# DLRM tower on one Trainium2 core: pairwise products in units of 64 samples instead of 32

## The chip, the cores and the metric

One core of one Trainium2 chip. The time is the device time of one execution in microseconds; the median over several runs counts, and less is better.

## The reference

2048 samples, each with 128 dense features and 26 ids into 26 tables of rows of 128 numbers. All in fp32. Per sample, the 26 looked-up rows and the dense row are multiplied with one another, and the products go through three layers:

```python
e = jnp.stack([tbl_0[ids[:, 0]], ..., tbl_25[ids[:, 25]]], axis=1)     # (2048, 26, 128)
sd = jnp.einsum('bfd,bd->bf', e, dense)                                # 26 products with the dense row
ss = jnp.einsum('bfd,bgd->bfg', e, e)
pairs = ss[:, iu, ju]                                                  # 325 pairs above the diagonal
z = jnp.concatenate([dense, sd, pairs], axis=1)
h = jnp.concatenate([z, dense], axis=1)                                # 607 columns
h = jnp.maximum(h @ W_top1 + b_top1, 0.0)                              # 512
h = jnp.maximum(h @ W_top2 + b_top2, 0.0)                              # 256
y = h @ W_top3                                                         # 1
```

## The kernel before

The 2048 samples are 16 tiles of 128, in four chunks of four tiles (`CHUNKS`). The last chunk (`LAST`) has an order of its own, written out by hand, in which its two halves (`EARLY`, `FINAL`) go through the layers one after the other.

Rows reach the core in two ways. Seventeen tables are **gathered**: POOL (GpSimd) issues one indirect DMA for each tile and table (L552), 16 x 17 = 272 in all, into the ring `rows` of 44 rows of 128 x 128. A tile takes 18 of them: the dense row, which SP loads, and 17 gathered ones. Before a gather overwrites a ring row, POOL waits until PE has turned it (`rows_turned`). The nine tables of 1000 rows are **looked up** by matmul: DVE makes one-hot columns from the ids (`one_hots`, L1113 in the first chunk, L1115 after it), into four slots, and PE multiplies them with a high and a low part of the table (`look_up`, L576 and L577), 72 blocks of two matmuls for each chunk, one chunk ahead.

PE turns a tile's rows by transposing them, four at a time, into two PSUM banks (`turn_rows`, L597), one tile ahead of the products. DVE or ACT copies them into `turned` (`copy_rows`, L403) and places the looked-up rows there too (`place_found`, L417). Then PE makes the products: for each group of four samples, four matmuls of 27 x 26 (`products`, L616), which write four strips of one PSUM bank. A **unit** is eight groups, 32 samples, 32 matmuls, 8 x 26 = 208 columns of the 512 of a bank; in the profile its matmuls have two records each. A tile has four units, which alternate between the banks `gram_bank0` and `gram_bank1`. `copy_products` (L374) brings a unit into `gram`: DVE from the one bank, ACT from the other. PE waits for that copy before it writes the bank again (`gram_copied`), and the copy waits for the unit (`gram_done`).

The order of the first three chunks is that of the loops `work_off`, one on each engine. On PE each of the 4 x 4 steps (tile `t`, step `u`) is: turn a share of the next tile's rows, make unit `u`, look up three or four blocks for the following chunk. `first_products` makes the very first unit of a chunk ahead of this loop. After the 16 steps PE turns the products by feature (`turn_products`, L644), which waits for all copies of `gram`, then turns the pairs by sample (`turn_pairs`, L657) and runs layers 1 and 2 (L664, L710), with further lookups and the first turns of the following chunk in between. Each engine works strictly in its written order. The waits count events from the start of the program, so `UNITS` (four units to a tile) stands in every one of those counts.

Of the kernel before, what the change touches and what calls it, by code (L numbers as in the profile page):

```python
# [65 lines left out]
UNIT = 8  # L66
UNITS = GROUPS // UNIT
COLS_TURNS = -(-LATER // TURN)
# [63 lines left out]
def turns_before(u):  # L132

    return range(-(-u * TURNS // UNITS), min(-(-(u + 1) * TURNS // UNITS), TURNS))

# [23 lines left out]
def dlrm_tower(nc, dense, ids, ids_t, tables, w1, b1, w2, b2, w3, out):  # L159
# [11 lines left out]
    with ExitStack() as ctx:  # L171
# [189 lines left out]
        def copy_products(engine, chunk, n):  # L361


            mine = int(engine is nc.scalar)
            copy = nc.scalar.copy if mine else nc.vector.tensor_copy
            if chunk.n == 0 and n < 2:

                engine.wait_ge(w2_lo_made, 1)
                engine.wait_ge(w1_lo_made, K1)

            engine.wait_ge(gram_done, chunk.first * UNITS + n + 1)
            of = gram_bank[mine][0:ACROSS, 0:UNIT * LATER].rearrange("p (k f) -> p k f", k=UNIT)
            room = n % (HALF * UNITS) if chunk is LAST else n
            copy(gram[0:ACROSS, room * UNIT:(room + 1) * UNIT, :], of).then_inc(gram_copied[mine], 1)  # L374
# [30 lines left out]
        def place_found(engine, chunk, t):  # L405
# [6 lines left out]
            if t >= 2:  # L412

                engine.wait_ge(gram_done, (chunk.first + t - 1) * UNITS)
# [143 lines left out]
        def _(pe):  # L558
# [41 lines left out]
            def products(chunk, t, u):  # L600
# [9 lines left out]
                n = t * UNITS + u  # L610

                pe.wait_ge(gram_copied[n % 2], UNITS + (chunk.first * UNITS + n) // 2)
                for k in range(UNIT):
                    for q in range(GROUP):
                        sample = turned[:, t % 2, u * UNIT + k, q * FEATURES:(q + 1) * FEATURES]
                        last = pe.matmul(gram_bank[n % 2][q * QUAD:q * QUAD + FEATURES, k * LATER:(k + 1) * LATER],  # L616
                                         sample, sample[:, 0:LATER], start=True, stop=True)
                last.then_inc(gram_done, 1)

            def turn_products(part, g):  # L620

                if g == 0:

                    for i in range(2):
                        pe.wait_ge(gram_copied[i], UNITS + (part.first + part.tiles) * UNITS // 2)
# [127 lines left out]
            def work_off(chunk, following):  # L753
# [3 lines left out]
                for t in range(TILES):  # L757
                    for u in range(int(t == 0), UNITS):
                        if t + 1 < TILES:
                            turn_rows(chunk, t + 1, turns_before(u))  # L760
                        products(chunk, t, u)
# [139 lines left out]
        def _(act):  # L901
# [50 lines left out]
            def work_off(chunk, following):  # L952
                for t in range(TILES):
                    for u in range(UNITS):
# [6 lines left out]
                        if u % 2:  # L961
                            copy_products(act, chunk, t * UNITS + u)
# [133 lines left out]
        def _(dve):  # L1096
# [52 lines left out]
            def work_off(chunk, following):  # L1149
                for t in range(TILES):  # L1150
                    for u in range(UNITS):
                        if u % 2 == 0:
                            copy_products(dve, chunk, t * UNITS + u)
# [159 lines left out]
```

## Time and profile before

| | |
|---|---|
| runs (three) | 378.31 us median, 378.0 to 378.87 |
| span of the profiled execution, first to last instruction | 376.5 us |
| median of the runs beside that span | 1.8 us more |
| PE matmul busy | 347.3 us, 92% |
| PE weight loads (beside the matmuls) | 273.7 us, 73% |
| DVE busy | 252.4 us, 67% |
| ACT busy | 187.5 us, 50% |
| POOL busy | 267.1 us, 71% |
| mean granted TensorE clock | 0.982 of 2.4 GHz |

The record lists no time of its own for the profiled execution beside its span. Busy time leaves out the issue of instructions and waiting. A row of the timeline gives start, duration, engine, line, operation, tiles and shapes; the bracket behind it is the engine's idle time just before, and what ended it. Where several instructions of one kind follow one another, they are one row with their count.

### The profile page before, as it was taken

To read this page: it belongs to the slowest core of one execution; us is meant where nothing else is said; L and a number is where in the kernel's file an instruction comes from. 1 tells how busy PE (TensorE), PEld (TensorE's weight loads), DVE (VectorE), ACT (ScalarE), POOL (GpSimd) and SP (SyncE) were. 2 spreads that over 40 slices of the span, in tenths; PEclk is the share of its full clock that TensorE was granted. 3 is DMA by queue.
4 is the path that set the end of the run, shared out by engine and by line. 5 is a ranking of instruction groups with operands and counts; after the bars stand their busy time and mean duration, and the time that the engine had idled before them with its cause. 6 is when DMAs were issued, how large, how long until landed. Compare 5 with 4: busy or idle time off the path is not lost.

```text
span 376.5 us, 12740 instructions
## 1 busy us (share of the span) xinstructions
PE 347.3 (92%) x5585; PEld 273.7 (73%) x5585; DVE 252.4 (67%) x501; ACT 187.5 (50%) x320; POOL 267.1 (71%) x279
## 2 busy tenths in 40 slices
PE   2899988999799999998999999986899999989987
PEld 0566666876578888876788888864678778779876
DVE  0799899886589735787788646884588672545241
ACT  3356777677113426767323347574214345524443
POOL 6777778777777777777777777777777777877200
PEclk9999999999899999999999999999899999969999
DMA  7998114333242332333432331342243221122100
GB/s 191 256 256 201 51 49 106 94 85 112 67 111 77 85 84 57 86 88 97 111 81 84 78 91 51 87 119 71 75 104 91 51 62 51 52 51 52 31 4 1
DMA packets 20111, 33.43 MB, mean 89 GB/s; under 512 B 7917, under 2 KB 10491, under 8 KB 20057
## 3 DMA queue, kind: packets, MB, share of 16 engines
q0 software_dynamic: 8704, 17.84, 18.4%
q1 hardware_dynamic: 11353, 14.78, 15.0%
q8 instruction: 44, 0.72, 0.8%
q14 instruction: 10, 0.08, 0.1%
HBM read 32.60 MB, written 0.01 MB: 87 GB/s over the span
## 4 chain that ended last, share of the span: by engine, by line
PE 70%; POOL 13%; issue 7%; DMA 5%; DVE 4%; ACT 1%; SPq 0%; DVEq 0%; ACTq 0%; POOLq 0%
POOL rows L552 13%; PE late_bank L576 10%; PE late_bank L664 10%; PE gram_bank L616 8%; PE late_bank L577 8%; PE turn_bank L597 6%; DMA rows<-in_tbl_dram,index 4%; PE gram_bank L576 3%; PE spare_bank L710 3%; PE gram_bank L577 3%; PE spare_bank L576 2%; PE spare_bank L880 2%; PE spare_bank L577 2%; PE turn_bank L577 1%; PE turn_bank L576 1%
## 5 line engine op out<-in xcount | busy, mean ns | idle before, releaser
L552 POOL DMA_INDIRECT rows<-in_tbl_dram,index x272 | 266.3, 979 | 83.9 <-issue 80.5
L1115 DVE TENSOR_TENSOR one_hot<-table_ids,row_number 125x512 fp32r<-125x512 int32 x216 | 134.8, 682 | 30.8 <-PE gram_bank L577 13.1
L403 ACT COPY turned<-turn_bank 128x512 f32<-128x512 f32 (+1 forms) x69 | 68.3, 1033 | 49.0 <-PE turn_bank L597 49.0
L576 PE MATMUL late_bank<-one_hot,table_hi 125*128 125x512 f32 x168 | 72.1, 429 | 1.9 <-DVE one_hot L1113 1.0
L577 PE MATMUL late_bank<-one_hot,table_lo 125*128 125x512 f32 x168 | 67.6, 403 | 0.0
L616 PEld LDWEIGHTS gram_bank<-turned 128*27 128x27 f32 x4096 | 45.3, 106 | 18.7 <-issue 14.1
L616 PE MATMUL gram_bank<-turned 128*27 128x26 f32 x4096 | 55.0, 193 | 2.3 <-DVE turned L417 1.4
L597 PE MATMUL turn_bank<-ident,rows 128*128 128x128 f32 x288 | 44.1, 277 | 12.5 <-DMA rows<-in_tbl_dram,index 11.5
L597 PEld LDWEIGHTS turn_bank<-ident,rows 128*128 128x128 f32 x288 | 35.1, 143 | 23.0 <-DMA rows<-in_tbl_dram,index 14.2
L576 PEld LDWEIGHTS late_bank<-one_hot,table_hi 125*128 125x128 f32 x168 | 32.5, 194 | 16.5 <-issue 5.3
L1113 DVE TENSOR_SCALAR one_hot<-looked_up,row_number_sb 125x512 fp32r<-125x512 f32 x72 | 32.8, 496 | 11.5 <-issue 6.3
L577 PEld LDWEIGHTS late_bank<-one_hot,table_lo 125*128 125x128 f32 x168 | 32.6, 194 | 6.1
L929 ACT ACTIVATE h_hi<-late_bank,b_sb 128x512 fp32r<-128x512 f32 (+1 forms) x18 | 11.1, 617 | 36.7 <-PE late_bank L664 29.9
L374 DVE COPY gram<-gram_bank 124x208 f32<-124x208 f32 x32 | 12.0, 374 | 25.6 <-PE gram_bank L616 25.4
L1146 DVE TENSOR_TENSOR h_lo<-late_bank,h_hi 128x512 fp32r<-128x512 f32 (+1 forms) x18 | 10.8, 599 | 25.2 <-ACT late_bank L929 25.2
L374 ACT COPY gram<-gram_bank 124x208 f32<-124x208 f32 x32 | 11.3, 354 | 32.4 <-PE gram_bank L616 32.1
L664 PE MATMUL late_bank<-input_hi,w_hi 117*128 117x512 f32 (+3 forms) x72 | 27.2, 378 | 0.1
L664 PE MATMUL late_bank<-input_hi,w_lo 117*128 117x512 f32 (+3 forms) x72 | 25.8, 359 | 0.0
L664 PE MATMUL late_bank<-input_lo,w_hi 117*128 117x512 f32 (+3 forms) x72 | 25.8, 358 | 0.0
L417 ACT COPY turned<-looked_up 128x1152 f32<-128x1152 f32 x10 | 23.9, 2394 | 0.0
L576 PE MATMUL spare_bank<-one_hot,table_hi 125*128 125x512 f32 x48 | 21.4, 445 | 0.3 <-DVE one_hot L1115 0.2
L576 PE MATMUL gram_bank<-one_hot,table_hi 125*128 125x512 f32 x48 | 19.5, 407 | 0.2 <-DVE one_hot L1115 0.2
(138 smaller groups left out, 460.5 us busy)
## 6 DMA issues: line engine op xcount, KB each, us to landing
table_ids<-in_ids_by_table_dram SPq DMA_DIRECT2D x27, 256.0 KB, 3.3
rows<-in_tbl_dram,index POOLq DMA_INDIRECT x272
turned<-in_tbl_dram SPq DMA_DIRECT2D x6, 448.0 KB, 12.1
looked_up<-in_tbl_dram SPq DMA_DIRECT2D x3, 448.0 KB, 5.6
rows<-in_r_dense_features_dram SPq DMA_DIRECT2D x16, 64.0 KB, 3.2
gram<-in_W_top_dram SPq DMA_DIRECT2D x1, 702.0 KB
gram<-in_W_top_dram SPq DMA_DIRECT2D x1, 512.0 KB
turned<-in_tbl_dram SPq DMA_DIRECT2D x6, 52.0 KB
```

The costliest lines, as they stand in the source:

```text
L374: copy(gram[0:ACROSS, room * UNIT:(room + 1) * UNIT, :], of).then_inc(gram_copied[mine], 1)
L403: copy(to[:, f0:f1], of).then_inc(rows_copied[n % 2], 1)
L417: copy(to, of).then_inc(placed, 1)
L552: pool.indirect_dma_start(out=rows[:, row % RING_ROWS, :], out_offset=None, in_=tables[f], in_offset=bass.IndirectOffsetOnAxis(ap=index[:, ...
L576: pe.matmul(bank, table_hi[:, s, k, :], hot, start=k == 0, stop=False)
L577: pe.matmul(bank, table_lo[:, s, k, :], hot, start=False, stop=k == K_ROWS - 1).then_inc(one_hot_used, 1)
L597: last = pe.transpose(turn_bank[n % 2][:, f - f0, :], rows[:, (tile * ROWS + f) % RING_ROWS, :], ident[:])
L616: last = pe.matmul(gram_bank[n % 2][q * QUAD:q * QUAD + FEATURES, k * LATER:(k + 1) * LATER], sample, sample[:, 0:LATER], start=True, stop ...
L664: last = pe.matmul(h1_bank(part, n), w[0:p, k, cols], x[0:p, k, samples_of(part)], start=k == 0 and x is input_hi and w is w1_hi, stop=k = ...
L710: last = pe.matmul(h2_bank(part, n), w[:, k, n * P:(n + 1) * P], h1_slot(x, part, k), start=k == 0 and x is h1_hi and w is w2_hi, stop=k = ...
L1113: last = nc.vector.tensor_scalar(hot, id_slot(s), row_number_sb[:, k:k + 1], None, ALU.is_equal)
L1115: last = nc.vector.tensor_tensor(hot, table_ids[0:RK, (chunk.n * LOOKUPS + s) % ID_SLOTS, 0:wide], row_number[0:RK, k:k + 1].broadcast_to( ...
```

## The change

In the first three chunks a unit becomes 16 groups: 64 samples, 64 matmuls, 416 columns of a bank. A tile has two units. The first goes to `gram_bank0` and is copied by DVE, the second to `gram_bank1` and is copied by ACT. PE makes the first in step `u` = 0 and the second in step `u` = 2; the steps 1 and 3 keep their turns and lookups. `LAST` keeps units of 32 samples. `products_before(tile)` counts the units up to a tile, for the waits.

```diff
+WIDE = 2
...
+def wide(chunk):
+
+    return 1 if chunk is LAST else WIDE
+
+
+def products_before(tile):
+
+    return min(tile, LAST.first) * UNITS // WIDE + max(tile - LAST.first, 0) * UNITS
...
-            engine.wait_ge(gram_done, chunk.first * UNITS + n + 1)
-            of = gram_bank[mine][0:ACROSS, 0:UNIT * LATER].rearrange("p (k f) -> p k f", k=UNIT)
+            engine.wait_ge(gram_done, products_before(chunk.first) + n + 1)
+            unit = UNIT * wide(chunk)
+            of = gram_bank[mine][0:ACROSS, 0:unit * LATER].rearrange("p (k f) -> p k f", k=unit)
             room = n % (HALF * UNITS) if chunk is LAST else n
-            copy(gram[0:ACROSS, room * UNIT:(room + 1) * UNIT, :], of).then_inc(gram_copied[mine], 1)
+            copy(gram[0:ACROSS, room * unit:(room + 1) * unit, :], of).then_inc(gram_copied[mine], 1)
...
-                n = t * UNITS + u
-
-                pe.wait_ge(gram_copied[n % 2], UNITS + (chunk.first * UNITS + n) // 2)
-                for k in range(UNIT):
+                unit = UNIT * wide(chunk)
+                n = t * (GROUPS // unit) + u
+
+                pe.wait_ge(gram_copied[n % 2], UNITS + (products_before(chunk.first) + n) // 2)
+                for k in range(unit):
                     for q in range(GROUP):
-                        sample = turned[:, t % 2, u * UNIT + k, q * FEATURES:(q + 1) * FEATURES]
+                        sample = turned[:, t % 2, u * unit + k, q * FEATURES:(q + 1) * FEATURES]
...
                         if t + 1 < TILES:
                             turn_rows(chunk, t + 1, turns_before(u))
-                        products(chunk, t, u)
+                        if u % WIDE == 0:
+                            products(chunk, t, u // WIDE)
                         look_up(following, blocks_after("unit", t, u))
...
-                        if u % 2:
-                            copy_products(act, chunk, t * UNITS + u)
+                        if u == WIDE:
+                            copy_products(act, chunk, t * UNITS // WIDE + 1)
...
-                        if u % 2 == 0:
-                            copy_products(dve, chunk, t * UNITS + u)
+                        if u == 0:
+                            copy_products(dve, chunk, t * UNITS // WIDE)
```

The first piece moved stands on PE, in the third chunk, from the last turn ahead of its fourth tile. `turn_bank` takes turned rows, `gram_bank` products, `late_bank` a lookup's sum; the brackets name semaphores waited for. Before:

```order
L597 MATMUL turn_bank1<-ident,rows 128x128 [waits rows_copied1,gathered2_4]
L597 MATMUL turn_bank1<-ident,rows 128x128
L616 MATMUL gram_bank1<-turned 27x26 [waits gram_copied1]
L616 MATMUL gram_bank1<-turned 27x26 x31
L576 MATMUL late_bank0<-one_hot,table_hi 128x512 [waits one_hot_made]
L577 MATMUL late_bank0<-one_hot,table_lo 128x512
L576 MATMUL late_bank0<-one_hot,table_hi 128x512 [waits one_hot_made]
L577 MATMUL late_bank0<-one_hot,table_lo 128x512
L576 MATMUL late_bank0<-one_hot,table_hi 128x512 [waits one_hot_made]
L577 MATMUL late_bank0<-one_hot,table_lo 128x512
L616 MATMUL gram_bank0<-turned 27x26 [waits found_placed,gram_copied0,rows_copied1,rows_copied0]
L616 MATMUL gram_bank0<-turned 27x26 x31
```

Changed (the lines of the file have moved by 12 to 14):

```order
L609 MATMUL turn_bank1<-ident,rows 128x128 [waits rows_copied1,gathered2_4]
L609 MATMUL turn_bank1<-ident,rows 128x128
L588 MATMUL late_bank0<-one_hot,table_hi 128x512 [waits one_hot_made]
L589 MATMUL late_bank0<-one_hot,table_lo 128x512
L588 MATMUL late_bank0<-one_hot,table_hi 128x512 [waits one_hot_made]
L589 MATMUL late_bank0<-one_hot,table_lo 128x512
L588 MATMUL late_bank0<-one_hot,table_hi 128x512 [waits one_hot_made]
L589 MATMUL late_bank0<-one_hot,table_lo 128x512
L629 MATMUL gram_bank0<-turned 27x26 [waits found_placed,gram_copied0,rows_copied1,rows_copied0]
L629 MATMUL gram_bank0<-turned 27x26 x63
```

The unit between the turn and the lookups is gone, its 32 matmuls now stand in the unit before, and the next tile's first unit has 64.

The second piece is ACT in the third chunk's first tile: copies of turned rows (L403, then L415), of products (L374, then L386), and the placing of looked-up rows (L417, then L429). Before:

```order
L403 COPY turned<-turn_bank1 128x4x4x32 [waits rows_turned,dense_split]
L374 COPY gram<-gram_bank1 124x208 [waits gram_done]
L417 COPY turned<-looked_up 128x9x4x32 [waits found_copied]
L403 COPY turned<-turn_bank0 128x4x4x32 [waits rows_turned,dense_split]
L403 COPY turned<-turn_bank1 128x2x4x32 [waits rows_turned,dense_split]
L374 COPY gram<-gram_bank1 124x208 [waits gram_done]
```

Changed:

```order
L415 COPY turned<-turn_bank1 128x4x4x32 [waits rows_turned,dense_split]
L429 COPY turned<-looked_up 128x9x4x32 [waits found_copied]
L415 COPY turned<-turn_bank0 128x4x4x32 [waits rows_turned,dense_split]
L386 COPY gram<-gram_bank1 124x416 [waits gram_done]
L415 COPY turned<-turn_bank1 128x2x4x32 [waits rows_turned,dense_split]
```

The two copies of products are one, behind the placing and one copy of rows.

The third piece is DVE in the third chunk's second tile, copies of products among one-hots. Before:

```order
L374 COPY gram<-gram_bank0 124x208 [waits gram_done]
L1115 TENSOR_TENSOR one_hot<-table_ids,row_number 125x512 [waits one_hot_used] x4
L1115 TENSOR_TENSOR one_hot<-table_ids,row_number 125x512 [waits one_hot_used,ids_loaded2]
L1115 TENSOR_TENSOR one_hot<-table_ids,row_number 125x512 [waits one_hot_used] x3
L374 COPY gram<-gram_bank0 124x208 [waits gram_done]
L1115 TENSOR_TENSOR one_hot<-table_ids,row_number 125x512 [waits one_hot_used] x4
```

Changed:

```order
L386 COPY gram<-gram_bank0 124x416 [waits gram_done]
L1129 TENSOR_TENSOR one_hot<-table_ids,row_number 125x512 [waits one_hot_used] x4
L1129 TENSOR_TENSOR one_hot<-table_ids,row_number 125x512 [waits one_hot_used,ids_loaded2]
L1129 TENSOR_TENSOR one_hot<-table_ids,row_number 125x512 [waits one_hot_used] x7
```

The second copy is gone, and twelve one-hots follow the first without a copy between them.

## Rows read from the trace of the kernel before

**Rows 1.** The page: busy shares, and the chain that ended last, by engine.

```profile
PE 347.3 (92%) x5585; PEld 273.7 (73%) x5585; DVE 252.4 (67%) x501; ACT 187.5 (50%) x320; POOL 267.1 (71%) x279
...
PE 70%; POOL 13%; issue 7%; DMA 5%; DVE 4%; ACT 1%; SPq 0%; DVEq 0%; ACTq 0%; POOLq 0%
```

**Rows 2.** Waits of POOL's gathers: us in total, times, longest.

```profile
POOL rows L552 <- issue: 80.5, 264, 0.3
POOL rows L552 <- PE turn_bank L597: 2.1, 7, 0.3
```

**Rows 3.** POOL in order of time: the first and last of 272 gathers.

```profile
2.68 1.10 POOL L552 DMA_INDIRECT rows<-in_tbl_dram,index  x1 [1.28 <-DMA index<-in_ids_dram]
...
350.65 0.95 POOL L552 DMA_INDIRECT rows<-in_tbl_dram,index  x1 [0.30 <-issue]
```

**Rows 4.** PE in order of time: turns that waited for gathers, and the last turn.

```profile
178.26 0.66 PE L597 MATMUL turn_bank<-ident,rows 128*128 128x128 f32 x4 [0.80 <-DMA rows<-in_tbl_dram,index]
...
265.07 1.09 PE L597 MATMUL turn_bank<-ident,rows 128*128 128x128 f32 x4 [3.57 <-DMA rows<-in_tbl_dram,index]
...
328.69 0.66 PE L597 MATMUL turn_bank<-ident,rows 128*128 128x128 f32 x4 [0.91 <-DMA rows<-in_tbl_dram,index]
...
331.23 0.69 PE L597 MATMUL turn_bank<-ident,rows 128*128 128x128 f32 x2 [1.21 <-DMA rows<-in_tbl_dram,index]
...
353.35 0.38 PE L597 MATMUL turn_bank<-ident,rows 128*128 128x128 f32 x2
```

**Rows 5.** The chain that ended last: its last piece that is not PE's, before 331.

```profile
328.65 2.53 DMA rows<-in_tbl_dram,index
```

**Rows 6.** Busy time by stretch (us; busy of each engine; PEclk; DMA share; GB/s).

```profile
331.30:353.40 22.10, 22.09 (x450) 20.12 (x451) 9.47 (x29) 9.57 (x30) 15.72 (x16) 0.87 0.21 54
353.40:376.50 23.10, 18.87 (x377) 16.16 (x375) 6.24 (x24) 9.32 (x32) 0.00 (x0) 1.00 0.01 3
```

**Rows 7.** PE in order of time, first chunk's fourth tile: lookup, unit, next unit.

```profile
105.98 0.39 PE L576 MATMUL late_bank<-one_hot,table_hi 125*128 125x512 f32 x1
106.21 0.40 PE L577 MATMUL late_bank<-one_hot,table_lo 125*128 125x512 f32 x1
106.54 0.98 PE L616 MATMUL gram_bank<-turned 128*27 128x26 f32 x64
...
109.04 0.98 PE L616 MATMUL gram_bank<-turned 128*27 128x26 f32 x64
```

**Rows 8.** PE in order of time: the last two units of the program.

```profile
357.23 0.40 PE L616 MATMUL gram_bank<-turned 128*27 128x26 f32 x26
357.79 1.02 PE L616 MATMUL gram_bank<-turned 128*27 128x26 f32 x96 [0.15 <-issue]
```

**Rows 9.** The page's costliest groups: one-hots and copies (busy us, mean ns | idle before).

```profile
L1115 DVE TENSOR_TENSOR one_hot<-table_ids,row_number 125x512 fp32r<-125x512 int32 x216 | 134.8, 682 | 30.8 <-PE gram_bank L577 13.1
...
L374 DVE COPY gram<-gram_bank 124x208 f32<-124x208 f32 x32 | 12.0, 374 | 25.6 <-PE gram_bank L616 25.4
...
L374 ACT COPY gram<-gram_bank 124x208 f32<-124x208 f32 x32 | 11.3, 354 | 32.4 <-PE gram_bank L616 32.1
```

**Rows 10.** DVE's copies of looked-up rows and the gathers under them; the four gathers' sum.

```profile
145.15 1.53 DVE L417 COPY turned<-looked_up 128x1152 f32<-128x1152 f32 x1 [1.04 <-ACT looked_up L914]
...
145.82 1.35 POOL L552 DMA_INDIRECT rows<-in_tbl_dram,index  x1 [0.30 <-issue]
...
323.96 1.89 POOL L552 DMA_INDIRECT rows<-in_tbl_dram,index  x1 [0.30 <-issue]
...
324.59 1.37 DVE L417 COPY turned<-looked_up 128x1152 f32<-128x1152 f32 x1
...
sum 6.80, POOL 6.21; mean POOL 1.55
```

**Rows 11.** Busy time by stretch, columns as in rows 6.

```profile
330.00:333.40 3.40, 2.19 (x70) 1.70 (x70) 1.61 (x4) 0.85 (x3) 2.75 (x3) 0.50 0.27 63
178.30:184.00 5.70, 5.70 (x179) 4.41 (x180) 4.07 (x9) 2.69 (x4) 4.17 (x6) 1.00 0.38 105
```

More of the change, by code:

```diff
@@ L412, in place_found @@
             if t >= 2:
-                engine.wait_ge(gram_done, (chunk.first + t - 1) * UNITS)
+                engine.wait_ge(gram_done, products_before(chunk.first + t - 1))
             to = turned[:, t % 2].rearrange("p i (q f) -> p f q i", q=GROUP)[:, ROWS:FEATURES]
@@ L624, in turn_products @@
                     for i in range(2):
-                        pe.wait_ge(gram_copied[i], UNITS + (part.first + part.tiles) * UNITS // 2)
+                        pe.wait_ge(gram_copied[i], UNITS + products_before(part.first + part.tiles) // 2)
                 if part.tiles == TILES:
```

## The prediction

> **What bounds the kernel now.** I read the share of busy time first, then what POOL (GpSimd) waits for, then POOL in order of time, and last the chain that ended last. The shares seem to name TensorE (PE): busy 92% of the span, and 70% of the chain [rows 1]. That is misleading. POOL issues 272 indirect gathers, one table row per sample each, and its waits say that 80.5 us of its idle time, 264 times at most 0.3 us, is "issue", the gap ahead of nearly every gather; only seven gaps, no longer than the others, are put down to PE [rows 2]. So a gather takes 0.95 us and 0.30 us of gap, and nothing holds POOL up from the first gather at 2.68 to the last at 350.65 us [rows 3]. 271 times 1.25 is 339 us; the other 9 us are longer gathers, spoken of below.
>
> PE runs after the gathers. It waits for rows at 178.26 us (second chunk) and at 265.07 us (third), and in the last chunk at 328.69 (0.91 us) and 331.23 us (1.21 us) [rows 4]. The chain says the same near its end: it comes down POOL's gathers to the one issued at 328.65 us, whose landing takes 2.53 us [rows 5], and from there it is PE. From 331.3 us on PE is busy 22.09 of 22.10 us until it turns the last gathered rows at 353.35 us, and the last 23.1 us hold nothing of the first three chunks [rows 4, 6].
>
> So the end is set by two things: **when the gather of 328.65 us is issued**, and the 45.3 us (331.23 to 376.5) of the last chunk's work behind its landing. The change edits neither.
>
> **The change, part by part.**
>
> *Fewer switches on PE.* In 12 tiles, four units of 32 products become two of 64: 24 fewer. In a tile without turns one unit starts at 106.54 and the next at 109.04 us: 2.50 us for a unit and six lookup matmuls [rows 7]. Before the unit, lookup matmuls follow one another at 0.23 us (six of them 1.40), so a unit costs 1.10 us; the gap ahead of it is 0.10 of that, 0.33 us after the last lookup instead of 0.23. Joining two units saves at least that gap, 0.10 us: the products themselves stay. The other end is from the place where two units already stand nearly side by side: 26 and 96 records in 1.58 us [rows 8], which is 1.66 us for the 128 of a pair, against 2 x 1.10 = 2.20: 0.54 us. I take 0.4, nearer to that row, because it is the same instruction in the same order. 24 times 0.4 is **9.6 us of PE** (2.4 to 13.0). All of it lies ahead of a wait for gathers. Three joined pairs stand behind the wait at 265.07 us; they save 1.2 us (0.3 to 1.6) and bring PE that much earlier to the rows of 328.69 and 331.23 us, so the two waits grow from 2.12 to about 3.3 us. On the time: 0.
>
> *Fewer, wider copies.* 24 copies of 208 columns by VectorE (DVE) at 0.374 us and 24 by ScalarE (ACT) at 0.354 become 12 and 12 of 416 columns [rows 9]. Their cost is not shown: no less than the old one, no more than twice it (0.75 and 0.71 us). I take the middle, 0.56 and 0.53: DVE and ACT save about 2 us each in three chunks, off the path. What waits for a copy: the next unit into the same bank, now a tile later, and the turn of the products behind the last tile, whose second unit is now made one step earlier. On DVE the copy stands ahead of the one-hots. Where eight lookups now follow one unit, PE wants the eighth one-hot behind seven lookups (seven times 0.47) and a turn of rows (0.66, as at 178.26 us [rows 4]): 3.9 us after the unit. Four one-hots are ready by then; the copy and four more take at most 0.75 + 4 x 0.68 = 3.5 us [rows 9]. So no new wait follows, and a small one would be paid from the 3.3 us above.
>
> *Order on ACT.* The copy of the second unit goes behind the placing of looked-up rows and two copies of turned rows. The placing needs looked-up rows and the tile before; nothing waits that did not. SP and POOL keep their order.
>
> **The sum.** The profiled execution has a span of 376.5 us; 0 from PE and 0 from the copies leave 376.5. The median of the runs, 378.31, is 1.8 us above that span; I carry this over: **378.3 us**. The three runs spread over 0.87 us, so 0.2% (0.76 us) is about what can be told from no change.
>
> **What can still move the end: the gathers' own pace.** Behind 62 us nearly all long gathers lie under DVE's copy of looked-up rows into `turned`. Four of these copies come ahead of 328.65 us; the gathers under them took 6.21 us together, 2.41 above four times 0.95 [rows 10]. The gather of 145.82 us began 0.67 us into the copy and took 1.35 (0.40 over); that of 323.96 had run for 0.63 us when the copy began and took 1.89 (0.94 over). The change leaves these copies alone, but PE reaches each about a microsecond earlier, which shifts them against POOL's period of 1.25 us. If all four came out like the cheap one: 1.60, the end 0.8 us earlier; all like the dear one: 3.76, the end 1.35 us later. They average 0.60 now, close to the middle (0.67), so I put the shift at 0.
>
> By the Trainium skill (SBUF — State Buffer, "Who interferes with whom") a DVE copy in a two-port mode blocks GpSimd for the whole instruction; at 1.37 us of copy for each of the four that would be up to 5.48 - 2.41 = 3.1 us later. No gather here lost more than 0.94, so the rows decide.
>
> **The rivals.**
>
> 1. *The gathers fall under DVE's copies* (slower). Place: the four copies above, one at the start of each of the last three chunks and one in the last chunk's middle. Price: up to +1.35 us, **379.7 us**. It decides once the four cost 3.17 us together (0.79 each). For it: one of the four is at the dear end, and all four move. Against: they would have to move the same way. 0.12. The same mechanism at its cheap end gives **377.5 us**: 0.06.
>
> 2. *PE really is the bound* (faster). Then the whole 9.6 us would show: **368.7 us**. For it: 92% busy, 70% of the chain. Against: POOL without a break, and PE waiting for rows in every chunk. 0.06.
>
> 3. *The longer waits cost TensorE its clock* (slower). During the waits of the last chunk the granted clock fell to 0.50, the 1.2 GHz level [rows 11], and behind 331.3 us it still averaged 0.87 over 22.1 us [rows 6], which is 5.7 us at the low level, 2.9 us of PE's work lost; it rose while PE was turning products without a gap. After the shorter wait at 178.26 us it stayed at 1.00 [rows 11]. If the low stretch began at 331.23 itself and not at 330.0, 1.2 us more would lie there: +0.6. If a like stretch came once more behind the last gather: +2.9. **379 to 381 us**. Against: what lies before 331.23 us is paid by waiting, and the work that resumes there is unchanged. Nothing is to be had the other way: the last gather, issued at 350.65 and landing 2.53 us later like the other, is there at 353.18, and PE at 353.35, so a clock that never fell would gain 0.17 us. 0.06.
>
> A rule of the Trainium skill speaks against the change here: by TensorE: Matmul & The Clock Gate, "HAM oscillation — how this bites in real kernels", bursts of matmuls parted by waits for DMA each run at the low clock. Were that so at every wait for gathers, rival 3 would be the likeliest; the full clock after 178.26 us speaks against it.
>
> **How the numbers follow.** No difference that can be told 0.70, gathers dearer 0.12, cheaper 0.06, PE the bound 0.06, clock 0.06. Faster by over 0.2%: 0.06 + 0.06 = 0.12. Slower: 0.12 + 0.06 = 0.18. The forecast's own band is 378.3 within 0.75. The range, 377.4 to 379.3, adds the cheap end of the gathers and most of the dear one; it leaves out rival 2 and the far ends of 1 and 3, together some 0.15.
>
> **What the new profile would show.** POOL unbroken, its idle time still "issue", its last gather within 1.3 us of 350.65. Units of 128 matmul records in 12 tiles, and a pair 0.1 to 0.5 us shorter than two units were. PE's waits for gathers longer by some 8 us in all, the two of the last chunk about 3.3 us together. The chain still on POOL's gathers ahead of 331 us. The prediction is wrong if POOL's stream ends over a microsecond earlier, if PE no longer waits near 331 us, or if the last 45 us have grown.

## The result, and the profile after

The changed kernel takes **380.43 us** (median of 22 runs), the kernel before on the same chip 378.32: ratio 1.0046, interval [1.0027, 1.0064]. The median is 2.1 us higher and the ratio says 0.46% slower, where no difference was forecast; the time is outside the range. Medians here and below are of all runs, while ratios leave out runs over 1.5% above the fastest of the same kernel (here 1719.87, 384.95 and 382.73 us). Without that of 1719.87 us, whose cause is not known, the runs spread from 377.0 to 385.0 us, where before had 377.2 to 379.3. The profiled execution has a span of 378.0 us, 1.5 more than before.

The page, with the shares, the chain and the groups that answer to [rows 1, 9]:

```profile
PE 345.5 (91%) x5585; PEld 274.9 (73%) x5585; DVE 249.5 (66%) x489; ACT 185.7 (49%) x308; POOL 266.8 (71%) x279
...
PE 87%; issue 6%; DVE 4%; ACT 1%; DMA 0%; SPq 0%; DVEq 0%; ACTq 0%
...
L629 PE MATMUL gram_bank<-turned 128*27 128x26 f32 x4096 | 55.0, 193 | 13.0 <-issue 8.7
...
L386 DVE COPY gram<-gram_bank 124x416 f32<-124x416 f32 (+1 forms) x20 | 10.1, 503 | 24.0 <-PE gram_bank L629 24.0
...
L609 PE MATMUL turn_bank<-ident,rows 128*128 128x128 f32 x288 | 44.3, 279 | 0.4 <-ACT turned L415 0.4
```

The same groups of TensorE before, from the list by line:

```profile
L616 PE MATMUL gram_bank<-turned 128*27 128x26 f32 x4096 | 55.0, 193 | 2.3 <-DVE turned L417 1.4
...
L597 PE MATMUL turn_bank<-ident,rows 128*128 128x128 f32 x288 | 44.1, 277 | 12.5 <-DMA rows<-in_tbl_dram,index 11.5
```

Three things are to be read here. PE is busy 1.8 us less, as it should be, but idle 3.3 us more (32.5 us in place of 29.2): that is the 1.5 us. The idle time ahead of the turns, 12.5 us and nearly all of it waits for gathers, is gone (0.4 us are left); in its place 13.0 us stand ahead of the products, where 2.3 were, and 8.7 of them are "issue", time in which PE waited for nothing that the profile shows. And POOL, 13% of the chain before, is no longer on it, although it works as before: its waits (L564 is the gather) and its last gather, which answer to [rows 2, 3], are

```profile
POOL rows L564 <- issue: 82.0, 269, 0.3
```

```profile
350.53 0.95 POOL L564 DMA_INDIRECT rows<-in_tbl_dram,index  x1 [0.30 <-issue]
```

So PE has become the bound. Where its new gaps lie, the order of time on PE shows. A unit of 64 samples has 128 records of L629; four of the 24 are broken:

```profile
74.31 1.39 PE L629 MATMUL gram_bank<-turned 128*27 128x26 f32 x112
...
77.97 0.31 PE L629 MATMUL gram_bank<-turned 128*27 128x26 f32 x16 [2.27 <-issue]
...
167.31 1.37 PE L629 MATMUL gram_bank<-turned 128*27 128x26 f32 x108
...
170.66 0.35 PE L629 MATMUL gram_bank<-turned 128*27 128x26 f32 x20 [1.98 <-issue]
...
180.00 0.61 PE L629 MATMUL gram_bank<-turned 128*27 128x26 f32 x49 [1.63 <-issue]
...
265.16 0.40 PE L629 MATMUL gram_bank<-turned 128*27 128x26 f32 x27 [2.01 <-issue]
...
359.59 1.02 PE L629 MATMUL gram_bank<-turned 128*27 128x26 f32 x96 [0.78 <-issue]
```

The fifth gap is in the last two units of the program, which the change leaves alone; it is the 0.15 us of [rows 8], grown to 0.78.

What happened in the first gap is told by the transfers of that moment. The page lists a queue of its own for "instruction": 44 transfers, 0.72 MB, so 16 KB each. TensorE's stream has 5585 matmul and 5585 weight-load records and some 180 waits; that is 258 of them to a transfer, so about 256 instructions to a **piece** of the program. The DMA view of 71.9 to 75.5 us has no packet of this queue, that of 75.5 to 78.0 us has one:

```profile
q8 instruction: 1, 0.02, 2.3%
```

In the records behind this row the transfer starts at 75.56 us; PE goes on at 77.97, 2.41 us later. Counted from the program's start in instructions, all five gaps stand at place 192 or 193 of 256, where a new piece begins. For each of these pieces the time from the start of its transfer to its first product is 2.25 to 2.51 us. **Theory A** is therefore: a product takes four instructions (two records, two weight loads), a joined unit 256 of them in 1.6 us at the pace of the first row above (1.7 to 2.1 us as units come, the broken ones apart); that is a whole piece in less time than the next one needs to arrive. Before, 128 instructions were followed by lookups, a matmul each 0.23 us [rows 7], and pieces arrived under them. Of 33 transfers between 60 and 310 us, 23 started behind the start of a lookup matmul before and 4 behind that of a product; now 16 of 32 start behind that of a product. **Rival B** is that the copies do it (a bank that is released late, VectorE or ScalarE in another order).

### The profile page after: what moved, and what is told of

Same layout as the page of the kernel before. It is cut to its first block, busy times and chain, and to the rows that moved or that the text cites. A ratio compares the mean times of both kernels' runs of the same rounds, so it can differ in the third digit from the quotient of the medians.

```text
span 378.0 us, 12716 instructions
## 1 busy us (share of the span) xinstructions
PE 345.5 (91%) x5585; PEld 274.9 (73%) x5585; DVE 249.5 (66%) x489; ACT 185.7 (49%) x308; POOL 266.8 (71%) x279
## 4 chain that ended last, share of the span: by engine, by line
PE 87%; issue 6%; DVE 4%; ACT 1%; DMA 0%; SPq 0%; DVEq 0%; ACTq 0%
PE gram_bank L629 14%; PE late_bank L677 11%; PE late_bank L588 11%; PE late_bank L589 10%; PE turn_bank L609 8%; PE spare_bank L588 4%; PE spare_bank L723 3%; PE spare_bank L589 3%; PE gram_bank L588 3%; PE gram_bank L589 3%; PE spare_bank L894 2%; DVE one_hot L1129 2%; PE row_number L723 2%; PE late_bank L735 1%; PE turn_bank L588 1%
## 5 line engine op out<-in xcount | busy, mean ns | idle before, releaser
L564 POOL DMA_INDIRECT rows<-in_tbl_dram,index x272 | 266.0, 978 | 84.1 <-issue 82.0
L415 ACT COPY turned<-turn_bank 128x512 f32<-128x512 f32 (+1 forms) x69 | 68.7, 1037 | 49.3 <-PE turn_bank L609 48.4
L589 PE MATMUL late_bank<-one_hot,table_lo 125*128 125x512 f32 x168 | 69.1, 412 | 1.1 <-issue 1.1
L629 PE MATMUL gram_bank<-turned 128*27 128x26 f32 x4096 | 55.0, 193 | 13.0 <-issue 8.7
L629 PEld LDWEIGHTS gram_bank<-turned 128*27 128x27 f32 x4096 | 45.3, 105 | 26.6 <-issue 22.9
L609 PEld LDWEIGHTS turn_bank<-ident,rows 128*128 128x128 f32 x288 | 36.7, 146 | 9.1 <-issue 1.4
L386 DVE COPY gram<-gram_bank 124x416 f32<-124x416 f32 (+1 forms) x20 | 10.1, 503 | 24.0 <-PE gram_bank L629 24.0
L429 ACT COPY turned<-looked_up 128x1152 f32<-128x1152 f32 x10 | 24.3, 2425 | 0.0
L928 ACT COPY looked_up<-late_bank 128x512 f32<-128x512 f32 x21 | 12.1, 593 | 20.8 <-PE late_bank L589 20.8
L589 PE MATMUL spare_bank<-one_hot,table_lo 125*128 125x512 f32 x48 | 19.9, 414 | 0.0
```

What stands on the lines that cost most here:

```text
L415: copy(to[:, f0:f1], of).then_inc(rows_copied[n % 2], 1)
L429: copy(to, of).then_inc(placed, 1)
L564: pool.indirect_dma_start(out=rows[:, row % RING_ROWS, :], out_offset=None, in_=tables[f], in_offset=bass.IndirectOffsetOnAxis(ap=index[:, ...
L589: pe.matmul(bank, table_lo[:, s, k, :], hot, start=False, stop=k == K_ROWS - 1).then_inc(one_hot_used, 1)
L609: last = pe.transpose(turn_bank[n % 2][:, f - f0, :], rows[:, (tile * ROWS + f) % RING_ROWS, :], ident[:])
L928: nc.scalar.copy(looked_up[:, s, 0:width(chunk)], bank).then_inc(found_copied, 1)
```

## The experiments

**1. The copies alone.** PE makes 32 products, looks up and makes the other 32, as before, but into one bank, with one wide copy behind the second half.

```diff
...
-                n = t * (GROUPS // unit) + u
...
-                pe.wait_ge(gram_copied[n % 2], ...)
-                for k in range(unit):
...
+                n, half = (t * UNITS + u) // w, u % w
...
+                if half == 0:
+                    pe.wait_ge(gram_copied[n % 2], ...)
+                for k in range(UNIT):
...
-                        if u % WIDE == 0:
-                            products(chunk, t, u // WIDE)
+                        products(chunk, t, u)
```

> Only the copies of the change: PE makes its products in steps of 32 samples as before, two steps into one bank, and one copy of 416 columns follows the second. If the change lost its time to PE's instruction supply in the long runs of 64 products (theory A), no gap inside a unit is over 0.4 us, PE waits for gathers near 331 us again, and the time is that of before, 378.3 within 0.8 us. If it lost it to the wide copies, to their later place on ACT and DVE or to the shared bank (theory B), the time stays near that of the change, 380.4, and PE's idle time lies ahead of units or of the turn of the products. If the gathers under DVE's copies cost it (theory C), POOL's last gather is issued later than in before by the time lost.

Measured: 378.23 us, ratio 1.0002 [0.9984, 1.0021]. The waits of this kernel are those of before again (turns on gathers, products on almost nothing):

```profile
PE turn_bank L609 <- DMA rows<-in_tbl_dram,index: 10.4, 9, 2.7
...
PE gram_bank L631 <- issue: 0.4, 1, 0.4
```

The wide copies cost nothing and save nothing. Here they come a step later than in the changed kernel, so the order of the copies is left to experiment 2.

**2. The long run alone.** 64 products in a row, but into two banks and with the narrow copies of before, in their old order. PE waits for both banks ahead of the 64.

```diff
...
-                        products(chunk, t, u)
+                        if u % 2 == 0:
+                            products(chunk, t, u)
+                            products(chunk, t, u + 1, ahead=True)
```

> Only the order of the change on PE: 64 products without a break, but as two units of 32 into the two banks, with the four narrow copies of before. Theory A (instruction supply): gaps of 1 to 2.5 us inside some units, 4 to 8 of them, put down to issue, and 380 us or more, spread widely over the runs. Theory B (copies): 378.3, PE waiting for gathers near 331 us. A fourth reading, that 6 to 8 lookups in a row find their one-hots late (theory D), gives 380 here too, but with PE idle on DVE's one-hots ahead of lookups instead of gaps inside units.

Measured: 380.0 us, ratio 1.0054 [1.0025, 1.0083], the changed kernel's loss. (Its profiled execution is a long one, 382.7 us of span.) The waits:

```profile
PEld gram_bank L619 <- issue: 24.8, 67, 2.8
...
PE gram_bank L619 <- issue: 10.5, 5, 2.7
```

Four gaps of 2.2 to 2.7 us inside joined units and one of 0.8 us in the last two units, all at place 192 or 193 of 256, are the 10.5 us. The waits for one-hots (theory D of the expectation) are small beside them: 2.9 us in this kernel, 1.4 before, and the longest, 1.41 us, ends 2.35 us behind the start of a transfer, so it may be the program as well. So the loss comes from the order of PE's instructions, and with the two experiments together B falls.

**3 and 4. Who sets the end?** Both kernels with 13 gathers less: the last gathered table is left out from the fourth tile on, and its products are made from what the ring held.

```diff
...
-                for n, f in enumerate(GATHERED):
+                for n, f in enumerate(GATHERED if t < RING_TILES else GATHERED[:-1]):
...
```

> The kernel before, without the gathers of the last gathered table from the fourth tile on: 13 gathers fewer, its products are made from what the ring held. If the gathers set the end of before, the gather that tile 14 waits for comes 11 x 1.25 = 13.75 us earlier, PE's waits for rows (11.9 us in all behind 91 us) go, then PE is the bound: 365 to 369 us. If PE is the bound already, 377 to 378.3.

> The changed kernel with the same 13 gathers left out. If PE has become the bound there by the gaps inside its units, it hardly gets faster: 378 to 380.4. If its end is still set by the gathers (theory C), it falls by some 11 us like the kernel before: 366 to 370.

Measured: before with 13 gathers less 365.49 us, ratio 0.966 [0.9622, 0.9698]; the changed kernel with 13 less 379.01, 1.0021 [0.9995, 1.0046] of before. The same edit takes 12.5 us from the one (377.96 on that chip) and about 1 from the other (1.0046 to 1.0021; the two intervals overlap). The last gather starts at 334.00 us in the one and, in the other, at

```profile
334.79 1.10 POOL L564 DMA_INDIRECT rows<-in_tbl_dram,index  x1 [0.30 <-PE turn_bank L610]
```

so POOL is done some 16 us earlier in both, and in the changed kernel gathers already wait for PE (9 of them, up to 1.8 us). The gathers set the end of the kernel before, as the prediction said; they do not set it any more.

These two kernels also show what the change costs PE. With 13 gathers less the waits for gathers are 1.1 us in the one and none in the other, so PE is the bound of both, and on this one chip the change takes it from 365.49 to 379.01 us: **13.5 us lost**. The gaps ahead of products, without and with the change, are

```profile
PE gram_bank L617 <- issue: 0.7, 1, 0.7
```

```profile
PE gram_bank L630 <- issue: 8.7, 5, 2.8
```

8.0 us more, in spans of 364.2 and 378.2 us. Another 2.5 us are put down to one-hots (3.7 us in place of 1.2; the longest such wait, 1.4 us, ends 2.27 us behind the start of a transfer and may be the program too), and PE is busy 2.2 us longer (346.2 in place of 344.0) at a mean granted clock of 0.977 in place of 0.991. In the full kernels the gathers hide most of this: the kernel before spends 12.5 us more than its PE needs, and the change uses that up.

**5. Does a stop let the piece in?** In the changed kernel, a wait that is already met after every fourth sample of a unit.

```diff
+                    if k % 4 == 0 and k > 0:
+                        pe.wait_ge(gram_copied[n % 2], ...)
```

> The changed kernel with a wait ahead of every fourth sample of a unit (15 more in each joined unit), on the semaphore and the value that the unit's first product has already waited for: they are met when they come, so no time is theirs by themselves. In the changed kernel's trace five gaps of 0.9 to 2.5 us stand inside units, at the instruction with which a new 16 KB piece of TensorE's program begins, 2.3 to 2.5 us behind the start of that piece's transfer. Theory A1 (TensorE's sequencer asks for the next piece only when something makes it stop, and a wait, even one that is met, is such a stop): the pieces are asked for early, the five gaps go, the pieces' transfers start inside units some hundred instructions ahead of the piece's end, and the time falls to 377.5 to 378.7 us. Theory A2 (a unit of 64 hands out 256 instructions in 1.6 us, less than a transfer takes, and it needs something that keeps TensorE itself busy for longer to get ahead of it): at least three of the gaps of over 0.8 us stay, at a piece's beginning again, and the time is 379.5 to 381 us.

Measured: 380.08 us, ratio 1.004 [1.0016, 1.0064]. The gaps stay, seven of 0.7 to 2.2 us (one of them in the last two units), at places 192 and 193 again, in order of time for instance

```profile
167.44 1.46 PE L631 MATMUL gram_bank<-turned 128*27 128x26 f32 x108
...
171.07 0.48 PE L631 MATMUL gram_bank<-turned 128*27 128x26 f32 x20 [2.17 <-issue]
```

A1 falls; A2 stands: a wait that is met is no help, PE has to be kept busy with something longer, as by the lookups of experiment 1.

**6. Half a piece later.** The changed kernel with 128 more instructions ahead, 32 small matmuls.

```diff
             spread_ids(0)
+            for _ in range(EXTRA):
+                pe.matmul(late_bank[0][0:RK, 0:LATER], ident[0:26, 0:1].broadcast_to([26, RK]), id_values[:, 0:LATER],
+                          start=True, stop=True)
             spread_ids(1)
```

> The changed kernel with 32 more small matmuls (26 columns, into a bank that the first look-up starts afresh) on TensorE's stream between its first two matmuls for the ids, where it was idle for 4.60 us: no work behind them is later, but every later instruction lies 128 instructions, half a 16 KB piece, further on in the program. Theory A (the gaps inside units are late pieces of the program): the gaps of over 0.8 us inside units stand again where a piece begins, at the place 192 or 193 modulo 256 counted from the start of the program, and so 32 samples away from where they stood within their unit (those at records 112, 52 and 96 of 128 leave these places), perhaps in other units; time 379 to 382 us. Rival C (the gaps belong to certain units, by what is on ScalarE, VectorE or the banks at that time): the gaps stand in the same units at the same records as before, at the place 64 or 65 modulo 256, and the time is that of the changed kernel, 380.4 within 0.5.

Measured: 392.19 us, ratio 1.028 [1.0228, 1.0333]. The time says nothing on the theories, for the expectation was wrong that the added matmuls are hidden: PE was idle there for 4.6 us, and they took 13.47 us.

```profile
5.46 13.47 PE L900 MATMUL late_bank<-table_ids,ident 26*125 26x26 f32 x64
...
96.82 1.25 PE L630 MATMUL gram_bank<-turned 128*27 128x26 f32 x92
100.63 0.25 PE L630 MATMUL gram_bank<-turned 128*27 128x26 f32 x6 [2.56 <-issue]
```

The places do say it. All eight gaps of over 0.5 us in joined units, and the one of 1.24 us in the last two units, stand at 192 or 193 again, the eight in other units than in the changed kernel: the third unit of the first chunk, which broke at record 112, is whole, and the fifth breaks (the rows above). Rival C falls.

With this run a pattern shows. Each joined unit holds the beginning of one piece. In the five kernels with joined units of one bank (the changed one, and experiments 4, 5, 6 and 11) every gap of over 0.45 us stands in a unit whose new piece begins at record 79 of 128 or later; no unit whose piece begins in the first 73 records has one. In the changed kernel those at 79, 101, 108 and 112 break, those at 80, 81 and 87 do not; at 80 and 87 it comes and goes from kernel to kernel. So a piece is late only where over half a unit, at its fast pace, lies right ahead of it; not every such piece is late.

**7 and 8. Can the gathers be sped up?** [Rows 10] show gathers that are longer beside VectorE's copies of looked-up rows. Here those copies are written as the larger of two equal inputs, in the kernel before and in that of experiment 1.

```diff
-            copy = nc.scalar.copy if engine is nc.scalar else nc.vector.tensor_copy
+            copy = nc.scalar.copy if engine is nc.scalar else lambda to, of: nc.vector.tensor_tensor(to, of, of, ALU.max)
```

> The kernel before, with VectorE's copy of found rows (128 x 1152, six of them) made as the larger of the rows and themselves. In the trace of before each of the six gathers that run beside such a copy is longer than the usual 0.95 us (1.35 to 1.89 us), 3.7 us in sum, and the tail behind the last gather is fixed. Theory G (the gathers set the end of the kernel before, and VectorE's copy within SBUF keeps GpSimd from writing its descriptors): the six gathers are of usual length, the last gather starts 2 to 3.7 us earlier, time 374.5 to 376.5 us. Rival H (the gathers beside these copies are longer for another reason, or any VectorE instruction of that size does it): the gathers stay long, time 377.8 to 378.8.

> The kernel of the earlier experiment that keeps TensorE's order of before (32 products, then look-ups) but gives 64 samples one bank and one copy, with VectorE's copy of found rows made as in the run beside it. By theory A its units are short enough for the program to arrive in time, so it follows the gathers as the kernel before does: with theory G 374.5 to 376.5 us, within 0.5 of the run beside it, since copies off the path give nothing. If the wide copies are worth something once the gathers are shorter (TensorE's waits for copied banks), it is 0.5 to 1 us faster than that run. If theory H holds, 377.8 to 378.8.

Measured: 383.26 us, ratio 1.0142 [1.0118, 1.0167], and 384.46, 1.016 [1.0137, 1.0183]. A miss, in the other direction: the instruction takes 2.31 us in place of 1.40, and the gather beside it ends only when it is over, 0.7 us behind it in these rows:

```profile
145.34 2.32 DVE L408 TENSOR_TENSOR turned<-looked_up 128x1152 f32<-128x1152 f32 x1 [1.04 <-ACT looked_up L914]
```

```profile
145.48 2.86 POOL L552 DMA_INDIRECT rows<-in_tbl_dram,index  x1 [0.30 <-issue]
```

All gathers together took 266.3 us before and 272.7 here; the 6.4 us are somewhat more than the 5.2 us by which the median grew. That is theory G's mechanism with the sign of the edit wrong. By the Trainium skill (SBUF — State Buffer, "Who interferes with whom") a VectorE instruction with two inputs in SBUF contends with a GpSimd instruction that reads SBUF; this run agrees, with 1.9 us lost by that gather. That it is a read which is held up, no run here shows.

**9. The last two copies on ScalarE** (kernel before).

```diff
                 copy_output(CLOSING)
+                place_found(act, LAST, 2)
...
                     relu1(EARLY, n)
+                    if n == 1:
+                        place_found(act, LAST, 3)
...
-                place_found(dve, LAST, 2)
...
-                place_found(dve, LAST, 3)
```

> The kernel before, with the found rows of the last chunk's third and fourth tile (L417 at 324.59 and 344.69 us) copied by ScalarE, in gaps where it is idle, in place of VectorE. Making VectorE's copies two-input instructions lengthened their six gathers to 2.2 to 2.9 us and the kernel by 5 us; so the gathers do set the end of the kernel before, and what VectorE does between two places of SBUF holds GpSimd up. No gather beside ScalarE's ten copies of the same shape is long. If both hold, the gathers at 323.96 (1.89 us) and 344.92 (1.60 us) take the usual 0.95 and the last one starts 1.6 us earlier: 376.3 to 377.2 us, ratio 0.994 to 0.998. If the tail is set by TensorE from there on, or ScalarE's later copies push something behind, 377.8 to 379.

Measured: **376.36 us**, ratio 0.9953 [0.9937, 0.997]. The gather that took 1.89 us at 323.96 [rows 10] takes 1.11 here, at 323.77, and the last one starts at 349.0 us in place of 350.65. As expected.

**10. The copies in thirds** (kernel before).

```diff
-            copy(to, of).then_inc(placed, 1)
+            step = LOOKUPS if engine is nc.scalar else LOOKUPS // 3
+            for s in range(0, LOOKUPS, step):
+                last = copy(to[:, s:s + step], of[:, s:s + step])
+            last.then_inc(placed, 1)
```

> The kernel before, with each of VectorE's six copies of found rows made in three pieces of 128 x 384. If GpSimd can write a gather's descriptors between two pieces, the six gathers lose less than the 3.7 us in sum of before, about a piece (0.45 us) at most each, 2.7 us in sum or less: 376.8 to 378 us. If a gather that has begun waits for all three pieces, its 3.7 us stay, or grow by the two added starts: 378 to 379 us.

Measured: **375.13 us**, ratio 0.992 [0.99, 0.994], more than expected. Most gathers beside the pieces are hardly longer than usual, and all gathers together took 262.3 us in place of 266.3. VectorE and POOL in order of time, and the gathers' group:

```profile
321.79 0.95 POOL L555 DMA_INDIRECT rows<-in_tbl_dram,index  x1 [0.30 <-issue]
321.88 1.73 DVE L419 COPY turned<-looked_up 128x384 f32<-128x384 f32 x3
...
323.04 1.05 POOL L555 DMA_INDIRECT rows<-in_tbl_dram,index  x1 [0.30 <-issue]
```

```profile
L555 POOL DMA_INDIRECT rows<-in_tbl_dram,index x272 | 262.3, 964 | 84.2 <-issue 79.2
```

The last gather starts at 346.95 us, 3.7 earlier than before, and the span is 2.9 us shorter. This version beats both kernels.

**11 and 12. The same thirds in the changed kernel, and in that of experiment 1.** The edit is that of experiment 10.

> The changed kernel with VectorE's six copies of found rows in three pieces of 128 x 384. In the kernel before the same edit took 2.7 us away, because the gathers set its end. Theory A (TensorE sets the end of the changed kernel, by stalls for its program inside the joined units): the gathers get shorter by the same 3 us and the time does not move by more than the units' stalls scatter, 379 to 381 us, the five or so gaps of 0.8 to 2.5 us inside units still there. If the changed kernel still follows the gathers in some chunk, it gains as before did, 377 to 378.5.

> The kernel with TensorE's order of before, 64 samples in one bank and one copy, and VectorE's copies of found rows in three pieces. With the gathers 3 us earlier, TensorE's waits for them are some 5 us in place of 12, so that TensorE is nearer to the end. If the change's wider copies save TensorE or the copies' engines anything on the path, it is 0.5 to 1.5 us below the narrow kernel with the same pieces (375.1): 373.6 to 374.6. If, as it stood without the pieces, the copies lie off the path, 374.6 to 375.6. The gaps inside its units stay at 0.2 us, but for one at the program's end.

Measured: the changed kernel with thirds 381.83 us, ratio 1.0099 [1.0066, 1.0131]: its last gather starts at 347.38 us, 3.2 us earlier, and nothing is gained. Why it lies above the changed kernel by itself was not looked into; in its profile four gaps of over 0.8 us stand inside units at the same places.

```profile
PEld gram_bank L632 <- issue: 20.7, 63, 2.7
...
PE gram_bank L632 <- issue: 8.5, 7, 2.6
```

The kernel of experiment 1 with thirds: 375.32 us, 0.9918 [0.9898, 0.9937], the same as with the narrow copies (375.13). With PE's waits for gathers down to 5.2 us the wide copies still give nothing. Its largest gap inside a unit is the one at the program's end (0.79 us).

## Why the prediction was wrong

**What bounded the kernel before: right.** Experiments 3, 9 and 10 move the gathers alone and the time follows: 12.5 us for 13 gathers less, 1.5 and 2.7 us for shorter ones.

**The step that failed is "Fewer switches on PE", its lower end.** "Joining two units saves at least that gap, 0.10 us: the products themselves stay." The term was 9.6 us of PE saved, 2.4 to 13.0; experiments 3 and 4, with the gathers out of the way, show 13.5 us of PE lost, 8.0 of them in gaps where PE waited for its program. No end below zero was given, and no row excluded a loss. Two things were off. In a tile without turns a pair now costs

```profile
101.95 1.92 PE L629 MATMUL gram_bank<-turned 128*27 128x26 f32 x128
...
106.79 1.96 PE L629 MATMUL gram_bank<-turned 128*27 128x26 f32 x128
```

4.84 us with its twelve lookups, against twice 2.50 [rows 7]: 0.16 us saved, in the two later chunks about 0.2, not 0.4. The other end, 0.54, came from a place that the kernel runs through once. Times 24 that is 4 to 5 us. And the products do not all come at that pace: four joined units have gaps of 1.6 to 2.3 us at a late piece of the program, 7.9 us together (8.7 with that of the last two units), and one of 1.14 us stands in the lookups behind a unit (at 163.68 us, "issue" again, 2.43 us behind the start of a transfer). The hint was in [rows 8] itself: that row, taken as the model of a long run, carries "0.15 <-issue". It was read as a small part of 1.58 us; it was the stall, at its mildest.

**Where PE's time was to go: right in kind, overrun in size.** The saving was to vanish in waits for gathers; instead the stalls used up those waits. By the last chunk PE was 4.6 us late: that chunk's first unit starts at 313.21 us in place of 308.57. Some of it came back. The turn at 331.23 us [rows 4] is at 334.18 now, that of 353.35 at 354.54, 2.95 and then 1.19 us late, because no wait for gathers stands there and the clock stays up. The stretches that answer to [rows 6], and two of the first chunk (columns as there):

```profile
334.20:354.50 20.30, 20.03 (x455) 18.40 (x450) 10.46 (x32) 9.55 (x30) 13.32 (x14) 1.00 0.20 52
354.50:378.00 23.50, 18.94 (x378) 16.24 (x376) 6.31 (x24) 9.32 (x32) 0.00 (x0) 1.00 0.01 2
75.70:79.00 3.30, 1.03 (x19) 0.88 (x19) 0.61 (x2) 0.42 (x1) 2.38 (x4) 1.00 0.19 48
79.00:82.40 3.40, 3.40 (x11) 2.72 (x10) 2.73 (x4) 0.10 (x1) 2.76 (x3) 0.50 0.23 58
```

The last 1.5 us are those 1.2 and 0.3 behind that turn, where the gap at 359.59 us alone is 0.6 larger.

**Fewer, wider copies: nearly right.** VectorE's take 10.1 us in place of 12.0, the 1.9 us that were forecast as "about 2", off the path (experiments 1 and 12). But "no new wait follows" does not hold everywhere. At the start of the first chunk VectorE now waits for the whole first unit, copies it, and only then makes the one-hot for which PE waits, 1.13 us that were not there before:

```profile
66.74 0.50 PE L588 MATMUL spare_bank<-one_hot,table_hi 125*128 125x512 f32 x1 [1.13 <-DVE one_hot L1129]
```

```profile
65.50 0.59 DVE L386 COPY gram<-gram_bank 124x416 f32<-124x416 f32 x1 [0.83 <-PE gram_bank L629]
66.01 1.27 DVE L1129 TENSOR_TENSOR one_hot<-table_ids,row_number 125x512 fp32r<-125x512 int32 x2
```

A wait for a one-hot, 1.01 us, stands once more at 257.30 us; there a piece of the program begins as well, and which of the two came last can't be told.

**Rival 1, the gathers' own pace: did not decide.** The last gather moved by 0.12 us. But the mechanism is real, and worth 2.7 us (experiment 10).

**Rival 2, PE is the bound: its half came true by the change itself.** PE bounds the changed kernel, by stalls that the kernel before did not have.

**Rival 3, the clock: in the last chunk the other way.** It is at 1.00 where it was 0.87. But three of the four stretches at 0.50, the 1.2 GHz level, now begin within 1.6 us behind a stall for the program, as the one at 79.00 us above, and PE is busy all through it. In the kernel before the low stretches began behind waits for gathers (at 97.9, 265.1 and 330.0 us, the last for 6.8 us), and what they cost was taken from the next wait or, in the last chunk, overlapped with gathers still to come. Both have 13.7 us of it in all, so no more of the clock is lost; that it is now lost on the path is argued from these places, and how much of the 2.1 us it makes was not separated from the stalls.

**Open.** Why a piece is asked for early in some stretches and late in others was not settled; A2 says only what did not help and what did. Moving the beginning of pieces into the first half of every unit, which the pattern of experiment 6 suggests, was not tried. The parts of the 13.5 us in experiments 3 and 4 are read from one profile each, and 1.3 of the 14.0 us between the spans are not accounted for. Nearly every joined unit has one to three pauses of 0.2 to 0.3 us between the starts of two records, at no fixed place; they are unexplained too.

## What to carry to other kernels

An engine's program is a stream with a rate of its own: where a change makes a long run of very short instructions, count them against the size of a piece and the time that one takes to arrive (here 256 instructions in 1.7 to 2.1 us against 2.3 to 2.5 us), and give the cost of joining a lower end below zero. Slower work mixed in between, such as the lookups here, is cover for that stream, not only a cost of switching. A cost on an engine that waits anyway stays hidden only up to the length of its waits (here 12.5 us). And when an engine that is not the busiest sets the end, look for what lengthens its instructions first: three copies in place of one gave 2.7 us, while saving work on the busiest engine gave none.

## What the runs showed of the hardware

- From the start of a transfer of TensorE's program to the first matmul behind it took 2.25 to 2.51 us at the six places of the changed kernel where PE stood waiting for it, and 2.2 to 2.9 us in the other kernels. By the Trainium skill (Runtime: NRT & Kernel Launch, "Instruction fetch mechanics") the program comes in blocks of 256 instructions, 16 KiB each, and crossing into the next is "mostly hidden". The traces agree on the size of a block; on its cost they differ, and decide: 1.6 to 2.3 us at four of the 24 joined units.
- Thirty-two matmuls with 26 columns into one place of a bank took 13.47 us, 0.21 us for a record (experiment 6), where the products, of the same 26 columns, come at 0.012 us (1.39 us for 112 of them, in the first broken unit above). What makes the difference was not tested.
- A gather beside a VectorE instruction within SBUF: beside a copy of 1.4 us it was 0.4 to 0.9 us longer [rows 10], beside thirds of it 0 to 0.1 (the rows of experiment 10; one at 62.47 us was 0.5 longer), beside a two-input instruction of 2.3 us 1.9 us, and beside ScalarE's ten copies of the same shape in the kernel before not at all, but for one of 0.13 us.
